# Layer 0's attention products computed graph by graph on 64 x 64 parts of TensorE

## The reference

```python
h = einsum('bnc,cf->bnf', x, W)
s1, s2 = h @ a1, h @ a2
e = leaky_relu(s1[:, :, None] + s2[:, None, :], 0.2) * mask
att = softmax(e, axis=2)                      # 64 x 64 for each graph
h_prime = einsum('bij,bjf->bif', att, h)      # the product that is changed
return elu(h_prime + beta * h)
```

## Time and profile before

| | us |
|---|---|
| median of 3 executions | 1415.73 |
| lowest, highest | 1414.88, 1416.86 |
| the execution that was profiled | 1413.15 |
| span of its profile, first to last instruction | 1410.9 |
| PE busy within the span | 1336.3 (95%) |
| PEld busy | 1134.6 (80%) |
| DVE busy | 1057.7 (75%) |
| ACT busy | 789.5 (56%) |
| POOL busy | 139.2 (10%) |

### The profile page before, as it was taken

How to read it: one execution, slowest core, us unless ns; L and a number is a source line. 1 busy time by engine, 2 the same in 40 slices (tenths; PEclk the granted TensorE clock), 3 DMA queues, 4 the chain that set the end, 5 groups by cost and what they waited for, 6 DMA issues and landing times.

```text
span 1410.9 us, 26776 instructions
## 1 busy us (share of the span) xinstructions
PE 1336.3 (95%) x10357; PEld 1134.6 (80%) x10357; DVE 1057.7 (75%) x2367; ACT 789.5 (56%) x1450; POOL 139.2 (10%) x196
## 2 busy tenths in 40 slices
PE   3688999999999999999999999999999999999896
PEld 3577888888888888888888888888888887888784
DVE  4768887787787777778777787878878786858455
ACT  2445656656565666556556665565665555564453
POOL 5101101100010110100111010011001010100000
PEclk9899999999999999999999999999999999999998
DMA  4001000010000000000000000000000000000000
GB/s 158 16 9 39 1 23 31 16 33 4 22 30 22 30 15 22 15 22 30 22 30 15 7 30 22 30 22 30 15 7 30 23 31 9 31 8 31 16 1 30
DMA packets 54653, 34.52 MB, mean 24 GB/s; under 512 B 34896, under 2 KB 51536, under 8 KB 54608
## 3 DMA queue, kind: packets, MB, share of 16 engines
q1 hardware_dynamic: 52800, 29.43, 6.9%
q0 software_dynamic: 1248, 3.94, 0.8%
q10 hardware_dynamic: 560, 0.52, 0.1%
HBM read 12.92 MB, written 8.39 MB: 15 GB/s over the span
## 4 chain that ended last, share of the span: by engine, by line
PE 70%; DVE 15%; ACT 7%; issue 4%; POOL 2%; DMA 1%; SPq 0%; ACTq 0%; POOLq 0%; DVEq 0%
PE banks L121 16%; PE banks L123 15%; PE banks L122 15%; PE banks L586 8%; PE banks L581 3%; PE banks L745 2%; ACT y L269 2%; PE banks L730 2%; PE banks L649 2%; PE banks L719 2%; DVE l_stats L241 1%; PE banks L847 1%; DVE l_r L2404 1%; DVE l_r L2397 1%; ACT banks L1511 1%
## 5 line engine op out<-in xcount | busy, mean ns | idle before, releaser
L1500 ACT ACTIVATE l_r<-banks,bias_r 128x512 f32<-128x512 f32 x90 | 61.7, 686 | 178.8 <-PE banks L123 178.8
L255 POOL TENSOR_TENSOR l_rstd<-l_mv,eps 128x4 f32<-128x4 f32 x48 | 23.4, 487 | 903.0 <-DVE l_mv L249 903.0
L1517 ACT ACTIVATE banks<-banks,bias_h 128x512 f32<-128x512 f32 x96 | 63.3, 659 | 60.5 <-PE banks L123 60.5
L2143 DVE TENSOR_TENSOR l_rh_lo<-l_r,l_rh_hi 128x512 fp32r<-128x512 f32 x90 | 61.6, 687 | 27.7 <-ACT l_rh_hi L1366 27.4
L2404 DVE SCALAR_TENSOR_TENSOR l_r<-banks,l_r 128x512 f32<-128x512 f32 x90 | 61.6, 686 | 26.6 <-ACT banks L1511 24.7
L1511 ACT ACTIVATE banks<-banks,bias_z 128x512 f32<-128x512 f32 x96 | 63.4, 661 | 25.8 <-PE banks L123 25.6
L269 ACT ACTIVATE y<-l_sum,l_offset,l_rstd 128x256 f32<-128x256 f32 x128 | 70.6, 592 | 7.2 <-DVE l_offset L263 7.1
L586 PE MATMUL banks<-adj_t,y 128*128 128x128 f32 x544 | 73.7, 286 | 0.2 <-ACT y L269 0.2
L121 PE MATMUL banks<-l_rh_hi,u_hi 128*128 128x512 f32 x180 | 73.8, 410 | 0.0
L2386 DVE SCALAR_TENSOR_TENSOR l_r<-l_r,l_h 128x512 f32<-128x512 f32 x60 | 40.8, 682 | 43.5 <-ACT l_r L1500 43.5
L586 PEld LDWEIGHTS banks<-adj_t,y 128*128 128x128 f32 x544 | 69.0, 201 | 4.4 <-issue 2.5
(11 more groups left out here) (294 smaller groups left out, 4324.8 us busy)
## 6 DMA issues: line engine op xcount, KB each, us to landing
x_tok<-in_x_dram SPq DMA_DIRECT2D x15, 512.0 KB, 3.3
l_res<-y SPq DMA_DIRECT2D x15, 512.0 KB, 2.9
out_dram<-l_res SPq DMA_DIRECT2D x15, 512.0 KB, 3.0
l_vpair<-l_vstage SPq DMA_DIRECT2D x32, 128.0 KB, 3.2
w_raw<-in_L_gnn_w_w_dram POOLq DMA_DIRECT2D x3, 512.0 KB, 10.5
qkv_raw<-in_L_gnn_w_qkv_dram POOLq DMA_DIRECT2D x1, 768.0 KB, 7.8
l_res<-in_x_dram SPq DMA_DIRECT2D x1, 512.0 KB, 14.9
u_raw<-in_L_gnn_u_w_dram POOLq DMA_DIRECT2D x2, 256.0 KB, 10.3
```

Of the source, the lines that this page charges most:

```text
L1500: nc.scalar.activation(own(u).r[:, m, :], rz(u)[:, m, :], ACT.Tanh, scale=0.5, bias=w.biases["r"][:, m:m + 1]).then_inc(s.r_ready.of(u), 1)
L1517: nc.scalar.activation(hv(u)[:, m, :], hv(u)[:, m, :], ACT.Tanh, bias=w.biases["h"][:, m:m + 1]).then_inc(s.hv_ready.of(u), 1)
L2143: return nc.vector.tensor_tensor(parts[1][:, k, :], bank, parts[0][:, k, :].bitcast(F32), ALU.subtract)
```

## The change

Three things change.

1. `l0_attend` computes each graph by itself: 64 x 64 weights (`b.att_t[q, t, q]`), 64 rows of `b.h`, and 64 partitions of the result. Of a unit's 4 matmuls with 128 x 128 weights and 256 columns, 8 with 64 x 64 weights and 256 columns are made. First graphs use rows and columns 0 to 63 of TensorE, second graphs 64 to 127, and they alternate. In half n the first graphs' results go to bank 2 + n, the second graphs' to the other one, so that two matmuls that may be under way together write different banks. Half 0 is thus the first graphs of tiles 0 and 1 and the second graphs of tiles 2 and 3; half 1 is the rest.
2. Ahead of half 1 TensorE waits until both last matmuls of half 0 have ended (`l0_hp_done`, now 4 a unit), since half 1 uses each bank from the other row group. Ahead of each half a semaphore instruction of its own is issued (`l0_swapping`), which carries the wait. Both `l0_add_h` of a unit, and ACT's `l0_take_att` of unit 1, wait for all 4.
3. In `Norm` the semaphore `eps_added` goes; `var_ready` counts both steps.

```diff
@@ Norm
-        self.var_ready = Signal(p, f"{name}_var_ready", 1)
-        self.eps_added = Signal(p, f"{name}_eps_added", 1)
+        self.var_ready = Signal(p, f"{name}_var_ready", 2)
@@ Norm.root
         pool.wait_ge(*self.var_ready.at(u, 1))
         nc.gpsimd.tensor_tensor(self.rstd[:, :], self.mv[:, :, 1], self.p.eps[:, :],
-                                ALU.add).then_inc(self.eps_added.sem, 1)
-        pool.wait_ge(*self.eps_added.at(u, 1))
+                                ALU.add).then_inc(self.var_ready.sem, 1)
+        pool.wait_ge(*self.var_ready.at(u, 2))
@@ Signals
-        self.l0_att_turned, self.l0_att_t, self.l0_hp_done = one("l0_att_turned", 1), one("l0_att_t", 1), one("l0_hp_done", 2)
+        self.l0_att_turned, self.l0_att_t, self.l0_hp_done = one("l0_att_turned", 1), one("l0_att_t", 1), one("l0_hp_done", 4)
+        self.l0_swapping = one("l0_swapping", 1)
@@ TensorE
         def l0_attend(u, n):
             if n == 0:
                 pe.wait_ge(*s.l0_att_t.at(u, 1))
-            for t in range(2 * n, 2 * n + 2):
-                ins = nc.tensor.matmul(half_bank(u, t), b.att_t[:, t, :], b.h[:, t, 0:DIM], start=True, stop=True)
-            ins.then_inc(s.l0_hp_done.sem, 1)
+            else:
+                pe.wait_ge(*s.l0_hp_done.at(u, 2))
+            pe.sem_inc(s.l0_swapping.sem, 1)
+            for i in range(2):
+                for g in range(PER_TILE):
+                    q = slice(g * NODES, (g + 1) * NODES)
+                    t = 2 * ((n + g) % 2) + i
+                    ins = nc.tensor.matmul(half_bank(u, t)[q, :], b.att_t[q, t, q], b.h[q, t, 0:DIM],
+                                           start=True, stop=True)
+                    if i == 1:
+                        ins.then_inc(s.l0_hp_done.sem, 1)
@@ ScalarE, l0_take_att
-                act.wait_ge(*s.l0_hp_done.at(0, 2))
+                act.wait_ge(*s.l0_hp_done.at(0, 4))
@@ VectorE, l0_add_h
-            dve.wait_ge(*s.l0_hp_done.at(u, n + 1))
+            dve.wait_ge(*s.l0_hp_done.at(u, 4))
```

## The result

| | before | after |
|---|---|---|
| median of 4 executions, us | 1415.31 | 1434.45 |
| lowest, highest | 1414.88, 1416.86 | 1433.62, 1435.47 |
| the profiled execution | 1413.15 | 1435.47 |
| span of its profile | 1410.9 | 1433.3 |
| one loop iteration in the trace | 83.03 | 84.27 |

The ratio is 1.0134 (95% interval 1.0118 to 1.0150): the change costs 19.1 us. The forecast was 13.8 more, 1429.5, with a range up to 1438. The sign and most of the mechanism were right, and the size was more than a quarter too small.

What follows compares the result with a forecast made beforehand. TensorE was taken to set the time of the 11 iterations. 11 x 0.85 = 9.4 us in the loop plus 4.4 outside made 13.8, so 1415.73 + 13.8 = 1429.5 us; range 1423 to 1438.

Steps and rivals of the forecast that it cites:

- Two parts at once, slots of 0.215: Attention products on TensorE: 16 passes run two at a time, 8 slots of 0.215 us, 1.72 again, nothing won.
- Rivals 1 and 2: Attention products: first, 4 slots fewer a unit, not slower, 6%; second, parts don't overlap, 1.72 us more a unit, 1457, 9%.
- The switches: TensorE entering and leaving the 64 x 64 part size around the products: 0.33 us a unit, no full drain assumed.
- The wait in the middle: TensorE between the two halves: last pass's tail 0.165, semaphore 0.12, bare weight load 0.05; 0.35 us in all, bounds 0.22 and 0.55.
- pair-to-pair gap of 0.7 to 0.75: Sign of being right: this gap in us between the first half's last pair and the second half's first pair.
- `l_v` and L581: DVE finishes `l_v` 1.14 us later in the loop; TensorE then waits a new 0.18 us at L581.
- the cost of a unit is 1.14 - 0.29 = 0.85: Loop unit: DVE's 1.14 us delay less 0.29 us of slack at L581 costs 0.85 us.
- ACT has 34 us idle an iteration and only shifts: ACT in the loop: its idle time lets its work move later, with no cost added to the sum.
- Outside the loop: Fill and drain, 4.4 us: unit 3 0.67 (PE only), unit 15 0.65, unit 2 0.85, unit 1 1.0, unit 0 1.2.
- the forecast's own bounds: Whole kernel, the forecast's own case: 1424.5 to 1435.3 us, given 65%; the high end takes a 0.55 wait and full drains.
- Rival 4: Loop, candidates: slack of `l_rh_lo` is used up and PE waits there, 0.3 us more in 11 iterations, 1433; 10%.
- Rival 3: Attention products: passes start only in program order, 5 slots a half, 0.43 us a unit, 6.9 in all, 1436.5; 8%.

## Why the prediction was right, and where its size was off

- **Two parts at once, slots of 0.215**: right. A half is 1.08 us, and 3 x 0.215 + 0.05 + 0.38 = 1.075 was forecast. Rivals 1 and 2 fall: nothing was saved, and the parts do overlap.
- **The switches**: right. Into the parts 0.32, out of them 0.31 and 0.34; 0.34 in all in the run with columns alone, 0.33 forecast. No full drain: a switch cost 0.09 to 0.10 us over a slot, as the earlier trace rows had it. "TensorEngine Tiling (Array Packing)", Key Properties, of the Trainium skill speaks of a drain; the trace has the new part start 0.08 us before the modelled end of the row ahead (1032.28 + 0.40, against 1032.60).
- **The wait in the middle**: the semaphore took 0.19 us, from the modelled end of half 0 to the first row of half 1, where 0.12 stood in the sum. That is the 0.07 by which TensorE's own part was larger (0.74 for 0.67). The pair-to-pair gap of 0.7 to 0.75, named as a sign, was wrong by the sum's own terms, which give 0.50; it was 0.57 (1032.60 + 1.08 - 0.38 = 1033.30 to 1033.87).
- **`l_v` and L581**: right within this 0.07. `l_v` was done 1.22 later for 1.14, TensorE at L581 0.90 for 0.85, a new wait there included.
- **What failed**: "the cost of a unit is 1.14 - 0.29 = 0.85", and behind it "ACT has 34 us idle an iteration and only shifts". The 0.29 us of slack is real at L581, but `l_v` has a second reader, `l_sum`, and behind it a chain over POOL and ACT that ends at TensorE's one wait in the iteration, L708, which the earlier trace rows named. A wait that exists already leaves no slack in the chain that ends it: here the delay of that chain was paid in full. The iteration costs 1.24, so 11 x 0.39 = 4.3 us were left out by this step, 3.3 by the medians. That ACT idles elsewhere is no cover: from `y` to `l_qk` it is continuous.
- **Outside the loop**: 6.4 for 4.4. In the traces 1.1 of it is the clock's second stretch, 0.7 the half of unit 1's products at the lower clock, and 0.3 the wait for `l_rh_lo` at unit 3, where "only PE's 0.67 counts" was forecast; for the clock the forecast allowed 0.2, in unit 0.
- **Luck in the range**: 1434.45 also lies within the forecast's own bounds, up to 1435.3. These were opened for a wait of 0.55 in the middle and for full drains at the switches. The wait cost 0.38 to 0.40, and the drains did not come; the missing slack, the clock and the wait at unit 3 filled the room in their place.
- **Rival 4**, a new wait of the candidates for `l_rh_lo` in each iteration, did not come: there TensorE waits at L718 and between the halves, and nowhere on L121 for `l_rh_lo`. Its mechanism came once, at unit 3, with the 0.3 us that it was priced at.
- **Rival 3**, passes in strict order: its 1436.5 is nearer to the measured time than the forecast, but its mechanism is not there. Halves would have lasted 5 slots, not 4, and the run in another order excludes a strict start even between matmuls far apart. The page "TensorE: Matmul & The Clock Gate", Part 3, The mechanism, of the Trainium skill, says that matmuls start in program order; for parts of the array that do not overlap these rows disagree, and the measurement decides.
- **POOL**: nothing, as forecast.

## What to carry to other kernels

When a step makes a result later, follow every reader of it, not only the next one on the bound engine, up to the waits that the profile already shows: a chain that ends in an existing wait, and has no idle time of its own on the way, passes each delay on in full, and a slack found at another reader does not lower the bill. The same wait tells where a gain lies: taking 0.5 us of work out of ACT's stretch ahead of it gave 0.45 us an iteration, with nothing done to TensorE. And splitting a product into parts of the array that run at the same time won nothing here, where half the array had been multiplying zeros and two of the four 64 x 64 parts were used in its place (all four at once were not tried); it costs two switches (0.34 us here), and the wait of TensorE for itself cost 0.38 with the old products and 0.40 with the new.

## What the runs showed of the hardware

- Parts of 64 x 64 that differ in rows and columns run side by side as those that differ in columns do: 8 passes of 256 columns in 1.08 us, at 0.215 us a pair, the same time a column as on the full array.
- TensorE starts a matmul on an idle part ahead of earlier ones in the program: four passes on one part, then four on the other, took 1.09 us for 1.08 alternating, and the fourth pass in the program started among the last two.
- A wait of TensorE for its own last matmul, carried by a semaphore instruction, lets the next pass start 0.19 us after that matmul's modelled end.
- In the fill, where TensorE idles for 3 to 5 us at a time, the granted clock behind such a pause was 0.50. Behind one and the same pause it stayed there for some 3 us in some of the kernels and for 5.6 in others, and where it was long, eleven transposed products that no edit touched cost 1.1 us more.
